# Splitting Y and adding rows before the attention pass of a four-layer graph network on one Trainium2 core

## What is computed

```python
h = (x @ W).reshape(n, HEADS, CH)
a_src = jnp.einsum('nhc,hc->nh', h, att_src)
a_dst = jnp.einsum('nhc,hc->nh', h, att_dst)
e = jax.nn.leaky_relu(a_src[src] + a_dst[dst], NEG_SLOPE)
e = jnp.exp(e - m[dst])
alpha = e / (s[dst] + 1e-16)
out = segment_sum(h[src] * alpha[:, :, None], dst) + bias
y = x + out            # then a layer norm with gamma and beta
```

## Time and profile before

| what | us |
|---|---|
| median of the 3 runs | 4735.81 |
| the runs | 4734.94 to 4755.01 |
| time of the profiled execution | 4763.33 |
| its span, from the first to the last instruction | 4761.2 |
| TensorE busy | 4240.2 (89%) |
| VectorE busy | 4055.6 (85%) |
| ScalarE busy | 3062.0 (64%) |
| GpSimd busy | 827.5 (17%) |

### The profile page before, as it was taken

How to read it: one execution, slowest core, us unless ns; L and a number is a source line. 1 busy time by engine, 2 the same in 40 slices (tenths; PEclk the granted TensorE clock), 3 DMA queues, 4 the chain that set the end, 5 groups by cost and what they waited for, 6 DMA issues and landing times.

```text
span 4761.2 us, 259988 instructions
## 1 busy us (share of the span) xinstructions
PE 4240.2 (89%) x103202; PEld 3795.6 (80%) x103202; DVE 4055.6 (85%) x6401; ACT 3062.0 (64%) x10437; POOL 827.5 (17%) x952
## 2 busy tenths in 40 slices
PE   1899999839999999499969999699999989999998
PEld 1677777639999999488869999588888868888887
DVE  7799999989999999899989999877767766767666
ACT  2899999802222222487779999666666656666665
POOL 2355555413333334000000000000000000000000
PEclk7999999969999999799989999899999989999999
DMA  1000000048888887000025555333333333333333
GB/s 55 2 2 2 2 2 2 2 117 280 276 281 277 280 277 255 15 0 0 0 67 144 147 143 146 89 98 96 98 97 98 97 87 101 99 100 99 101 96 83
DMA packets 305220, 501.36 MB, mean 105 GB/s; under 512 B 76918, under 2 KB 78454, under 8 KB 305126
## 3 DMA queue, kind: packets, MB, share of 16 engines
q1 hardware_dynamic: 303782, 499.39, 35.4%
q0 software_dynamic: 576, 0.52, 0.1%
q10 hardware_dynamic: 768, 0.16, 0.0%
HBM read 408.40 MB, written 91.57 MB: 105 GB/s over the span
## 4 chain that ended last, share of the span: by engine, by line
PE 44%; DVE 24%; issue 13%; ACT 13%; POOL 3%; DVEq 1%; DMA 1%; ACTq 0%; POOLq 0%; SPq 0%
PE PS L1535 20%; ACT arena L869 11%; PE PS L1528 9%; DVE arena L1844 7%; DVE arena L2454 4%; POOL arena L751 3%; PE PS L1327 3%; PE PS L1325 3%; PE PS L1343 2%; DVE arena L2288 2%; DVE arena L2293 2%; PE PS L1349 2%; PE PS L1566 1%; PE PS L1449 1%; PE PS L1464 1%
## 5 line engine op out<-in xcount | busy, mean ns | idle before, releaser
L1844 DVE TENSOR_TENSOR arena<-iotab,arena 128x1024 bf16<-128x1024 bf16 (+4 forms) x1887 | 1605.2, 882 | 188.5 <-PE PS L1535 166.7
L1076 ACT ACTIVATE arena<-PS 128x384 bf16<-128x384 f32 x2450 | 1004.1, 501 | 544.5 <-PE PS L1528 540.9
L1535 PE MATMUL PS<-arena 32*128 32x193 bf16 (+1 forms) x41552 | 998.2, 242 | 47.0 <-DVEq L2455 42.1
L1535 PEld LDWEIGHTS PS<-arena 32*128 32x128 bf16 x41552 | 840.5, 93 | 151.6 <-DVEq L2455 59.1
L869 ACT ACTIVATE arena<-PS,m 128x196 bf16<-128x196 f32 x1813 | 740.6, 445 | 22.0 <-PE PS L1184 21.9
L1528 PE MATMUL PS<-Hp,arena 128*128 128x192 bf16 (+1 forms) x4900 | 537.9, 249 | 35.3 <-DVE Hp L1688 35.0
L1045 ACT ACTIVATE arena<-PS,ewB 128x64 f32<-128x64 f32 x2450 | 526.4, 479 | 34.7 <-PE PS L1388 34.7
L1325 PE MATMUL PS<-Hp,arena 128*128 128x72 bf16 x7350 | 499.2, 198 | 42.1 <-DVE arena L2190 40.9
L1327 PE MATMUL PS<-arena 128*128 128x72 bf16 x7350 | 499.8, 198 | 0.0
L1528 PEld LDWEIGHTS PS<-Hp,arena 128*128 128x128 bf16 x4900 | 383.2, 99 | 146.0 <-issue 84.4
L930 ACT ACTIVATE arena<-arena 128x32 f32<-128x32 f32 (+1 forms) x294 | 68.3, 232 | 648.2 <-DVE arena L2205 645.3
(11 more groups left out here) (374 smaller groups left out, 8298.0 us busy)
## 6 DMA issues: line engine op xcount, KB each, us to landing
arena<-hots SPq DMA_DIRECT2D x735, 256.0 KB, 2.6
arena<-codes SPq DMA_DIRECT2D x245, 512.0 KB, 5.2
hots<-arena SPq DMA_DIRECT2D x245, 256.0 KB, 5.1
arena<-hots SPq DMA_DIRECT2D x147, 320.0 KB
arena<-codes SPq DMA_DIRECT2D x49, 640.0 KB, 5.4
hots<-arena SPq DMA_DIRECT2D x49, 320.0 KB, 5.4
rows_h<-Hn SPq DMA_DIRECT2D x4, 1568.0 KB, 9.2
rows_l<-Y SPq DMA_DIRECT2D x1, 1764.0 KB, 9.8
```

Of the source, the lines that this page charges most:

```text
L1076: act.activation(RG[ROW_BUFFER[g]][:, 2 * i:2 * i + 2, 0:RW], ps[PAIR_BANK[q]][:, 0:2 * RW].rearrange("p (k c) -> p k c", k=2), ACT.Copy). ...
L1535: last = pe.matmul(ps[2 + q][:, b * SW:b * SW + SW - o], one_hot[32 * q:32 * q + 32, b * P:(b + 1) * P], rows_of[32 * q:32 * q + 32, 0:SW ...
L1844: return dve.tensor_tensor(to.rearrange("p k (n t) -> p k n t", t=4), iota_of[:, 0:n].rearrange("p (n t) -> p n t", t=4)[:, None, :, :] .t ...
```

## The change

ScalarE and VectorE make the three parts of `Y` earlier, in turns. ScalarE copies `Y` to the first part when its work in the sort is done. VectorE subtracts after the 49 compares L1973. ScalarE copies the remainder to the second part. VectorE subtracts again just before it waits for the two matmuls of the check. GpSimd adds the bias row to `Hn` and the beta row to `X` right after its last work of the sort; VectorE waits for both after the attention pass. SP no longer waits for `s_begin` before `load_codes`, nor for `f_oht` before the first three loads.

```diff
             def load_codes():
-                sp.wait_ge(s_begin, 1)
-
                 def body(dx, first):
                     for g in range(NG):
-                        sp.wait_ge(f_oht, dx * NG + g + 1)
+                        if g >= 3 or not first:
+                            sp.wait_ge(f_oht, dx * NG + g + 1)
...
             untyped_codes(LASTW)
 
+            for to, n in ((Hn, 0), (X, 2)):
+                pool.tensor_tensor(to[:, :, :], to[:, :, :], rows[:, n, :][:, None, :].to_broadcast((P, WINDOWS, DIM)),
+                                   ALU.add).then_inc(s_rows, 1)
+
             pool.wait_ge(s_runs, 1)
...
             sort_body(WINDOWS + 1, 0, False, False, True)
+
+            y_parts = Hp[:, :, :].rearrange("p w (a c) -> p w a c", a=PARTS)
+            act.wait_ge(k_code, WINDOWS)
+            act.activation(y_parts[:, :, 0, :], Y[:, :, :], ACT.Copy).then_inc(s_y_bf, 1)
+            act.wait_ge(s_y_rest, 1)
+            act.activation(y_parts[:, :, 1, :], agg[:, :, :], ACT.Copy).then_inc(s_y_bf, 1)
 
             act.wait_ge(s_runs, 1)
...
             last.then_inc(k_oc, 1)
+            parts = Hp[:, :, :].rearrange("p w (a c) -> p w a c", a=PARTS)
+            dve.wait_ge(s_y_bf, 1)
+            dve.tensor_tensor(agg[:, :, :], Y[:, :, :], parts[:, :, 0, :], ALU.subtract).then_inc(s_y_rest, 1)
             dve.wait_ge(k_mi, 1)
...
             dve.sem_inc(s_statD, 1)
+            dve.wait_ge(s_y_bf, 2)
+            dve.tensor_tensor(parts[:, :, 2, :], agg[:, :, :], parts[:, :, 1, :], ALU.subtract).then_inc(s_y_low, 1)
             dve.wait_ge(s_statA, 2)
...
             dve.sem_inc(s_self, 1)
-            parts = Hp[:, :, :].rearrange("p w (a c) -> p w a c", a=PARTS)
-            link(dve.tensor_copy(parts[:, :, 0, :], Y[:, :, :]))
-            link(dve.tensor_tensor(agg[:, :, :], Y[:, :, :], parts[:, :, 0, :], ALU.subtract))
-            link(dve.tensor_copy(parts[:, :, 1, :], agg[:, :, :]))
-            link(dve.tensor_tensor(parts[:, :, 2, :], agg[:, :, :], parts[:, :, 1, :], ALU.subtract))
-            link(dve.tensor_tensor(Hn[:, :, :], Hn[:, :, :], along(0), ALU.add))
             dve.wait_ge(s_pself, 1)
             pself = ns[:, 1, :, :]
             w4d = wide.rearrange("p w (h c) -> p w h c", h=HEADS)
             dve.tensor_tensor(w4d, Y[:, :, 0:DIM].rearrange("p w (h c) -> p w h c", h=HEADS), bc(pself, CH), ALU.mult)
             link(dve.tensor_copy(agg[:, :, DIM:WV], pself))
-            link(dve.tensor_tensor(X[:, :, :], X[:, :, :], along(2), ALU.add))
+            dve.wait_ge(s_y_low, 1)
             dve.sem_inc(s_begin, 1)
...
+            dve.wait_ge(s_rows, 2)
             link(dve.reciprocal(ns[:, 0, :, :], agg[:, :, DIM:WV]))
```

More of the change, by code:

```diff
@@ L407, in gnn_stack @@
         s_self, s_pself, s_t0, s_th = sem("s_self"), sem("s_pself"), sem("s_t0"), sem("s_th")
+        s_y_bf, s_y_rest, s_y_low, s_rows = sem("s_y_bf"), sem("s_y_rest"), sem("s_y_low"), sem("s_rows")
         s_sums = sem("s_sums")
```

## The result

The changed kernel took 4724.8 us (median of 12 runs, 4722.3 to 4728.9), the kernel before 4736.8 in the same comparison (12 runs, 4733.5 to 4757.5). The ratio is 0.9969, with a 95% interval of 0.9959 to 0.9980. The medians differ by 12.0 us, the forecast was 16.3; the time lies in the range, and within 0.5% of before, as forecast. Two of the 12 runs of before, 4755.0 and 4757.5, stand apart; without them its median is 4735.9 and the difference 11.1. The changed kernel's profiled execution took 4724.2 us, its span is 4722.3.

The account below looks back on a forecast made before the run. The prediction took the serial stretch between edge sort and attention pass as bound by VectorE. Moved work 18.9 plus early codes 5.0 less GpSimd's hold 7.6 gave 16.3 us, so 4735.8 - 16.3 = 4719.5 us; range 4707 to 4738.

Parts of the forecast that it names:

- Moved work: VectorE between sort and start signal: 22.4 us removed, 3.1 and 0.4 added, so the signal comes 18.9 us sooner.
- the first subtraction: After the 49 compares: its 3.83 us lie inside VectorE's 4.17 us wait for matmuls L1259, costing nothing.
- the second: Second subtraction, before L2005: takes 3.83 us, covers 0.74 us of waiting, leaves 3.1 us on the path.
- the exponent: ScalarE L949: VectorE now waits for it, 0.4 us, between 0.3 and 0.8.
- The hold by GpSimd: After the sort, two GpSimd additions of 5.2 us each hold L1961 and L1963; VectorE's chain 7.6 us late, bounds 0 to 15.8.
- Early codes: At the attention pass's start, first compare 0 to 1 us after the signal, not 5.4; gain 5.0 us, between 4.4 and 5.4.
- The sum: Whole kernel: 18.9 + 5.0 - 7.6 = 16.3 us less.
- The base: Savings worked out on a profiled execution of 4763.3 us, 27.5 above the 4735.8 median, were subtracted from that median unchanged.
- no block: Rival 1: VectorE's 32-partition operations pass beside GpSimd's additions; gain 23.9 us, time 4711.9; chance 0.13.
- not 9.3: Rival 2: each GpSimd addition takes 9.3 us, a dearer block; gain 8.1 us, time 4727.7; chance 0.12.
- the codes come too late: Rival 3: first codes come no sooner, queued behind the table's rows or issued late by SP; gain 11.3, time 4724.5; chance 0.09.
- the fourth rival: Attention pass start: TensorE's clock returns one window later, gain gone, or two windows later, 4754 us; chance 0.06.

Follow-up runs that it names:

- y_late_few: Changed kernel with the left-over-edges compare moved to group 2 and Y's split back on VectorE at its old place; median 4746.0 us of 12 runs.
- before_again: The kernel before, unchanged, run again for a second profile; 12 runs, median 4744.0 us, the profiled one 4742.0 us in the short rhythm.

## Why the prediction was right, and where a term was off

- **Moved work**: 18.9 us forecast. A and the X addition give 8.4, with 10.5 lost to the additions: 18.9. The split of `Y` alone, taken back in y_late_few, was worth 11.9, and 11.8 by the working. Its parts hold too: the first subtraction hidden (0.43 us of the wait left), the second 3.8 on the path with no wait left before the two copies from PSUM, the exponent 0.49.
- **The hold by GpSimd**: the mechanism, the two operations that it strikes and their order came as forecast. Its size was the term that was off. "I take 5.2" for one addition: it takes 6.85 and 6.82 with nothing in its way, 2.18 ns an element. Nearly all of the 1.65 us that are missing is the slope between the two sizes of L751, 1.65 ns where 2.18 is right (0.53 x 2456 = 1.3 us); the rest is the 0.66 us that was deducted. With 6.9 the same working gives 11.0, and the traces give 10.5 (4.50 + 5.96). The Trainium skill, "GPSIMD Engine Reference", section 3.1, has 4497 ns for 2048 elements, 2.2 ns each: here the page was right and the estimate from rows was not.
- **Early codes**: 5.0 forecast (4.4 to 5.4). The fourth one-hot comes 3.6 to 4.4 sooner, since VectorE needs 1.1 us to get into the pass, whatever the codes do, where 0 to 1 was forecast. 6.8 us from the end of the first compare to the fourth came as forecast (6.7). In the changed kernel none of it is given back later: its pass from the fourth compare on takes 850.0 us, that of before_again 850.5.
- **The sum**: 18.9 + 4.0 - 10.5 = 12.4, where 16.3 was forecast and 12.0 (12.5 in one rhythm) measured.
- **The base**: the profiled execution of before lay 27.5 us above the median, and the prediction took differences from it. That held, because all terms lie outside the pass; 19.2 of its C were the long rhythm (869.7 - 850.5). A difference read over the whole span would have been wrong by this much, and the two outliers of before also make the ratio, 0.9969, look better than the medians, 0.9975.
- **The rivals**: no block fell to L1971 and L1973. The additions took 7.0 and not 9.3. Distance B excludes that the codes come too late. Of the fourth rival a part came. TensorE's clock was back at the full level at 1024.2, but TensorE then stood for 2.65 us up to 1030.6, and from 1031.0 to 1037.8 the clock was at 0.50 again. The stretches read: length, busy us and count of PE, PEld, DVE, ACT and POOL, granted clock, DMA share, GB/s.

```profile
1028.00:1032.00 4.00, 1.40 (x30) 1.41 (x30) 3.83 (x7) 0.24 (x1) 1.04 (x1) 0.88 1.09 356
1032.00:1036.00 4.00, 3.22 (x57) 3.06 (x55) 4.00 (x8) 0.62 (x3) 2.67 (x2) 0.50 0.98 363
```

before_again has such a second spell as well (1046.6 to 1050.0), and the pass from the fourth compare on is no longer in the changed kernel than there. So the clock cost the change nothing that these traces show.

## What to carry to other kernels

Work given to GpSimd was free only where VectorE meanwhile did nothing of the kinds that were held here, operations with two inputs in SBUF and most tensor_scalars. A chain of tiny dependent operations was poor company, for one of 0.18 us can wait for a whole large instruction (6.14); the 49 compares were worse still, with 13.1 us against 10.5. Put such work beside VectorE's copies out of PSUM and reductions: here that alone was worth 8.2 us in the trace and 10.8 in the medians, beside 12.5 for the whole change. Before two traces are compared over a whole span, compare the period of the loops in each; one profiled execution may be in another rhythm than the median.

## What had not been expected of the hardware

- A pass of 49 windows has two stable rhythms, 17.28 and 17.64 us, by the order in which one GpSimd addition and one VectorE compare are issued; 17 to 20 us for the pass. Moving the compare by one group removes the long one. How often the long one comes differs between sets of runs of one kernel, from none of 23 to 5 of 12.
- Operations on 32 partitions are held like those on 128, and a tensor_scalar of 4 elements a partition waits 1.9 us; scans and sums with one input in PSUM, copies out of PSUM and reductions are not held. Nor are tensor_scalars of one element a partition: L1738 to L1740 of the kernel before keep 0.15 us at 47.88 to 48.40, beside two of GpSimd's instructions L617 (46.51 to 48.70).
- A fill, which only writes, holds a tensor_scalar (2.24 us instead of 0.18) and not an operation with two SBUF inputs (0.35). The Trainium skill, "SBUF — State Buffer", section "Who interferes with whom", says that an operation with two SBUF inputs contends with a GpSimd instruction that reads SBUF, not with one that only writes it, and names tensor_scalar among those that can enter a mode that contends with GpSimd; these rows agree.
- In seven of nine traces with early loads the first window of the pass is longer than the rest, by up to 5.4 us. In three of them the pass loses 5 to 6 us by it, most of it in one wait of TensorE for its own instructions, and the changed kernel is not one of the three. The cause is open.
